# Adjacency blocks of a graph network: one-hots of one chunk between additions, weightings of four chunks, addresses read by threes

## The reference

```python
deg = jnp.maximum(segment_sum(ones, dst, 1250), 1.0)
x = x + L0(relu(layernorm(x)), src, dst, deg)               # mean over neighbours, two linear maps
x = x + L1(relu(layernorm(x)), edge_weight)                 # two graph convolutions
x = x + L2(relu(layernorm(x)), edge_attr_128)               # a message for each edge, summed, then a GRU
x = x + L3(relu(layernorm(x)), edge_weight1)                # weighted sum over neighbours, a linear map
```

## Time and profile before

| | |
|---|---|
| median of 3 runs | 1490.85 us (1489.72 to 1490.96) |
| profiled execution | 1488.92 us |
| its span in the profile | 1486.7 us |
| busy in the span | PE 88%, DVE 66%, POOL 48%, ACT 38% |
| mean granted clock of TensorE | 0.957 of full speed |
| first one-hot of the build to its last addition's start | 294.86 to 539.62 us |

### The profile page before, as it was taken

One profiled execution on the slowest core, in us unless ns is written; L12 is line 12 of the kernel. 1 busy time (PEld: TensorE's weight loads), 2 busy tenths in 40 slices (PEclk: granted clock), 3 DMA queues, 4 the chain that ended last, 5 costly groups with the idle time before them and its releaser, 6 DMA issues.

```text
span 1486.7 us, 19898 instructions
## 1 busy us (share of the span) xinstructions
PE 1309.6 (88%) x4184; PEld 685.9 (46%) x4184; DVE 988.1 (66%) x1719; ACT 565.0 (38%) x1438; POOL 719.2 (48%) x873
## 2 busy tenths in 40 slices
PE   5859898098888888959998899999998999997998
PEld 2534443043333333438874444444454444443775
DVE  8798253078888889841286388888896576667432
ACT  0211311066666620121011388888886221222210
POOL 0677777677777725766771266676663000000000
PEclk9989999599999999979999999999999999998999
DMA  8832522110000044443223577777775000000220
GB/s 337 322 118 65 191 66 79 46 57 18 19 21 16 9 181 156 121 154 96 89 81 127 161 224 215 228 227 225 227 221 184 20 1 0 1 0 18 71 89 34
DMA packets 87236, 167.86 MB, mean 113 GB/s; under 512 B 16108, under 2 KB 44654, under 8 KB 84628
## 3 DMA queue, kind: packets, MB, share of 16 engines
q1 hardware_dynamic: 59044, 102.19, 20.4%
q0 software_dynamic: 25472, 59.97, 13.2%
q10 hardware_dynamic: 2672, 5.11, 1.1%
HBM read 115.97 MB, written 51.25 MB: 112 GB/s over the span
## 4 chain that ended last, share of the span: by engine, by line
PE 45%; issue 17%; POOL 14%; DMA 13%; DVE 9%; POOLq 1%; ACT 1%; DVEq 1%; ACTq 0%
PE pb L1060 21%; DMA arena<-p_rows,gidx 11%; POOL cell_rows L671 8%; PE pb L1142 6%; PE pb L1168 6%; PE pb L1328 5%; PE pb L1176 2%; POOL tiles L725 2%; PE pb L1046 1%; POOL arena L725 1%; PE pb L1083 1%; PE pb L1258 1%; DMA cell_rows<-tiles,gidx 1%; DVE arena L1560 1%; POOL arena L784 1%
## 5 line engine op out<-in xcount | busy, mean ns | idle before, releaser
L784 POOL DMA_INDIRECT arena<-p_rows,gidx x184 | 191.5, 1041 | 67.3 <-issue 58.4
L717 POOL DMA_INDIRECT dst_rows<-ering,gidx x168 | 172.2, 1025 | 100.0 <-issue 71.4
L671 POOL DMA_INDIRECT cell_rows<-tiles,gidx x168 | 168.8, 1004 | 68.0 <-issue 39.7
L1258 PE MATMUL pb<-arena 128*128 128x512 f32 x368 | 191.6, 604 | 5.6 <-ACT arena L944 5.6
L1576 DVE TENSOR_TENSOR arena<-pb,arena 128x384 f32 x272 | 150.0, 552 | 45.8 <-PE pb L1142 24.4
L1060 PE MATMUL pb<-ws,tiles 128*128 128x512 f32 (+1 forms) x360 | 146.3, 554 | 12.0 <-ACT tiles L806 12.0
L1684 DVE TENSOR_TENSOR arena<-pb,arena 128x512 f32<-128x512 f32 x184 | 124.4, 686 | 41.6 <-DMA arena<-p_rows,gidx 39.5
L1142 PE MATMUL pb<-arena 128*128 128x384 f32 x272 | 107.5, 520 | 47.9 <-POOL arena L725 46.1
L847 ACT ACTIVATE arena<-iota,free 128x128 f32<-128x128 f32 x272 | 94.3, 393 | 123.4 <-PE pb L1142 82.4
L1142 PE MATMUL pb<-tiles,arena 128*128 128x384 f32 x272 | 106.2, 514 | 22.8 <-POOL tiles L725 21.0
L1060 PE MATMUL pb<-arena,tiles 128*128 128x512 f32 x240 | 103.9, 593 | 0.0
(11 more groups left out here) (258 smaller groups left out, 2129.8 us busy)
## 6 DMA issues: line engine op xcount, KB each, us to landing
dst_rows<-arena SPq DMA_DIRECT2D x6, 2046.0 KB, 17.5
ering<-in_edge_attr_dram SPq DMA_DIRECT2D x41, 256.0 KB, 3.0
arena<-adj SPq DMA_DIRECT2D x10, 640.0 KB, 3.8
arena<-dst_rows SPq DMA_DIRECT2D x24, 264.0 KB
arena<-wt_gru SPq DMA_DIRECT2D x48, 128.0 KB
ws<-dst_rows SPq DMA_DIRECT2D x22, 264.0 KB, 2.9
arena<-in_x_dram SPq DMA_DIRECT2D x18, 256.0 KB, 8.7
arena<-in_L_gnn_W_hh_dram SPq DMA_DIRECT2D x3, 1024.0 KB
```

Of the source, the lines that this page charges most:

```text
L671: nc.gpsimd.indirect_dma_start(cell_rows[:, :], bass.IndirectOffsetOnAxis(gidx[:, SPAN * a + k:SPAN * a + k + 1], 0), cring[:, a, k], None ...
L717: nc.gpsimd.indirect_dma_start(dst_rows[:, :], bass.IndirectOffsetOnAxis(gidx[:, k:k + 1], 0), ering[:, k, :], None).then_inc(e_scattered[ ...
L784: nc.gpsimd.indirect_dma_start(rows[:, k, :], None, p_rows[:, :], bass.IndirectOffsetOnAxis(gidx[:, k:k + 1], 0)).then_inc(g_landed[k], 16)
L1258: nc.tensor.matmul(e_bank(k)[:], erowT[:, k % 4], w1e_sb, start=True, stop=True).then_inc(edge_mm, 1)
```

## The change

One-hots are made one chunk at a time, eight ahead, one after each addition, and compared with a copy of the row 1 to 128 in PSUM bank 4 (`counting`), which nothing else uses during the build. DVE's loop runs over 16 chunks. Its addresses are read one at the start and then five times three, each behind an addition. POOL weights four chunks (`HALF`) in one instruction of 128 x 1024, and PE waits for it once in four chunks. A column is scattered after every second turn instead of in each; `EARLY` is 2, so 16 columns are scattered in the build and 152 behind it.

```diff
-EARLY = CELL_CHUNKS // TURN // COL
+HALF = TURN // 2
+EARLY = CELL_CHUNKS // TURN // (2 * COL)
...
             def weights_turn(i, with_column=None):
-                for q in range(TURN // 2):
-                    pool.wait_ge(dst_hot, TURN // 2 * i + q + 1)
+                for q in range(2):
+                    pool.wait_ge(dst_hot, TURN * i + HALF * (q + 1))
                     passed()
-                    hot = ohd(2 * q, 2)
...
+                    hot = ohd(HALF * q, HALF)
...
-                    if q == 1 and with_column is not None:
-                        scatter_column(with_column)
+                if with_column is not None:
+                    scatter_column(with_column)
...
-                    weights_turn(COL * i + k, k)
+                    weights_turn(2 * COL * i + 2 * k, k)
+                    weights_turn(2 * COL * i + 2 * k + 1)
...
                         if k % 2 == 0:
                             pe.wait_ge(src_hot, TURN // 2 * i + k // 2 + 1)
-                            pe.wait_ge(weighted, TURN // 2 * i + k // 2 + 1)
+                        if k % HALF == 0:
+                            pe.wait_ge(weighted, 2 * i + k // HALF + 1)
...
-            def hots(i, q):
-
-                at_least(dve, block_done, TURN * i + 2 * q - 6)
-                vtt(ohd(2 * q, 2)[:, :, 0], iota1[:].unsqueeze(1).to_broadcast([P, 2, P]),
-                    cellm[:, bass.ds(TURN * i + 2 * q, 2), 1:2].to_broadcast([P, 2, P]), ALU.is_equal).then_inc(dst_hot, 1)
+            def hot(i, k):
+
+                vtt(ohd(k % TURN, 1)[:, :, 0], counting.unsqueeze(1),
+                    cellm[:, bass.ds(2 * TURN * i + k, 1), 1:2].to_broadcast([P, 1, P]), ALU.is_equal).then_inc(dst_hot, 1)
...
             def turn(i, last):
-                at = table_values(cell_at[0:1, bass.ds(TURN * i, TURN)], (CELLS - 1) * P)
...
+                at = list(table_values(cell_at[0:1, bass.ds(2 * TURN * i, 1)], (CELLS - 1) * P))
+                for k in range(2 * TURN):
+                    add_block(i, k, at[k])
+                    if k % 3 == 0 and len(at) < 2 * TURN:
+                        at += table_values(cell_at[0:1, bass.ds(2 * TURN * i + k + 1, 3)], (CELLS - 1) * P)
+                    if not last or k < TURN:
+                        hot(i, k + TURN)
+
+            counting = pb[4][:, 0:P]
+            link(nc.vector.tensor_copy(counting, iota1[:]))
```

More of the change, by code:

```diff
@@ L720, in weights_turn @@
             def weights_turn(i, with_column=None):
-                for q in range(TURN // 2):
-                    pool.wait_ge(dst_hot, TURN // 2 * i + q + 1)
+                for q in range(2):
+                    pool.wait_ge(dst_hot, TURN * i + HALF * (q + 1))
                     passed()
-                    hot = ohd(2 * q, 2)
-                    nc.gpsimd.tensor_tensor(hot[:, :, 1:3], hot[:, :, 0:1].to_broadcast([P, 2, 2, P]),
-                                            cellm[:, bass.ds(TURN * i + 2 * q, 2), 2:4].unsqueeze(3).to_broadcast([P, 2, 2, P]),
+                    hot = ohd(HALF * q, HALF)
+                    nc.gpsimd.tensor_tensor(hot[:, :, 1:3], hot[:, :, 0:1].to_broadcast([P, HALF, 2, P]),
+                                            cellm[:, bass.ds(TURN * i + HALF * q, HALF), 2:4].unsqueeze(3).to_broadcast([P, HALF, 2, P]),
                                             ALU.mult).then_inc(weighted, 1)
-                    if q == 1 and with_column is not None:
-                        scatter_column(with_column)
+                if with_column is not None:
+                    scatter_column(with_column)
             def weights_and_edges(i):
@@ L742, in _ @@
                 weights_and_edges(i)
-            for i in range(COL * EARLY, CELL_CHUNKS // TURN):
+            for i in range(2 * COL * EARLY, CELL_CHUNKS // TURN):
                 weights_turn(i)
@@ L1570, in add_block @@
             def add_block(i, k, at):
-                n = TURN * i + k
+                n = 2 * TURN * i + k
                 dve.wait_ge(block_done, n + 1)
@@ L1578, in turn @@
             def turn(i, last):
-                at = table_values(cell_at[0:1, bass.ds(TURN * i, TURN)], (CELLS - 1) * P)
[L1580 to L1584, removed]
+                at = list(table_values(cell_at[0:1, bass.ds(2 * TURN * i, 1)], (CELLS - 1) * P))
[7 more added lines that the diff above has]
+            link(nc.vector.tensor_copy(counting, iota1[:]))
             dve.wait_ge(cells_loaded, 16)
             dve.wait_ge(wt_stored[0], 32)
-            turns = CELL_CHUNKS // TURN
-            for q in range(3):
-                hots(0, q)
+            turns = CELL_CHUNKS // (2 * TURN)
+            for k in range(TURN):
+                hot(0, k)
             turn(0, False)
```

## The result

| | before | changed |
|---|---|---|
| median (range), us | 1490.41 (1489.72 to 1490.96) | 1510.24 (1507.93 to 1511.71) |
| profiled execution, us | 1488.92 | 1510.29 |
| its span, us | 1486.7 | 1508.6 |
| first addition, us | 298.95 | 299.65 |
| last addition, us | 539.62 | 558.92 |

The ratio of the times is 1.0132 (95% interval 1.0114 to 1.0149): **slower**, by 19.8 us, where 7 us of gain were forecast. The last addition stands 19.3 us later, so nearly all of the loss arises in the build. Here are DVE's three kinds of work in the build by line, in the changed kernel (ns min/median/max, first and last start), with POOL's weighting behind them. They answer to the earlier trace rows.

What follows compares the result with a forecast made beforehand. DVE's row of additions was taken to set the build's pace; 298.95 + 1.0 + 229.2 + 3.4 put the last addition at 532.6 instead of 539.62, 7.0 us earlier, so 1484.0 us, range 1472 to 1493.

Steps and rivals of the forecast that it cites:

- Addresses by threes: DVE's address reads in the build: a read of three words was to take 0.39 us, bounds 0.30 and 0.60.
- An interval with a read: Between DVE additions with a three-word read and a one-hot between them: forecast 0.94 us, five a round.
- plain intervals: Between DVE additions with only a one-hot between them: forecast 0.75 us, ten a round.
- The chain's extra waits: Build, chain through one-hot, POOL's weighting and PE, 4.13 us: forecast to add 0.2 us a round, 3.4 in all.
- a read has a floor: Rival, DVE's address reads: three words cost 0.60 us like eight, 14.5 us added, time 1498.5; chance 0.10.
- One-hots of one chunk: DVE in the build: 272 one-hots instead of 136, 0.29 us each, wholly within time that was waited.
- The 1510 us: Time by the skill's instruction-cost table if none of the one-hots' 26 us more of DVE were covered.
- The row in PSUM: DVE's one-hots in the build: a PSUM source frees them from POOL, so 0.2 to 0.4 us lost a turn goes.
- the rival in which it does not: Rival: PSUM source does not free one-hots from POOL; up to 1 us each, some 60 us, 1545; chance 0.04.
- Weighting by fours: POOL in the build: one weighting of 1024 columns was to take 2.06 us, with next to no fixed part.
- The first rival: DVE's reads short or hidden: 1474, or near 1469 if the 4.13 us chain sets a round of 12.7; chance 0.12.
- The late columns: Sixteen columns moved behind the build: forecast to cost nothing, 7 us to spare; rival that they surface, 1484 to 1492, chance 0.04.

## Why the prediction was wrong

**The step that failed** is the price in "Addresses by threes": "by a line between them three take 0.39", with bounds of 0.30 and 0.60 from the reads of one and of eight words. Three words measured 0.745, above the upper bound. The line assumed that a read costs more with each word, from one to eight, at one rate. The runs show 0.22 for each further word wherever a read takes no whole group of four, and 0.04 for all three further words where it does. Eight words at 0.60 were cheap for their number, which fits two whole groups. Two points of the earlier trace rows could not show this, and the upper end was no bound: a read of fewer words can cost more than one of eight, which the forecast took as excluded without a reason in the rows.

Most of the working around this price held. An interval with a read was to be 0.12 + read + 0.17 + 0.26; with 0.745 that is 1.30, and the first one measured 1.30, the later ones 1.22 and 1.23. The second is longer, 1.40, for a longer read (below). Five such intervals take 6.37 us instead of 4.70, in 17 rounds 28.4 us. The rest of a round moved little: ten plain intervals sum to 7.57 instead of 7.50 (17 x 0.07 = 1.2 more), and its start takes 1.26 instead of 1.36 (1.7 less). That start is the read and 0.94 more in every kernel with single one-hots, from 1.25 with a read of 0.31 to 1.54 with one of 0.60; the forecast had 1.06 more. Rounds in which single intervals are longer than these medians add 2.0: together 17 x (15.32 - 13.56) = 29.9. The chain's extra waits of 3.4 us vanished, as longer intervals cover them, and the first addition came 0.7 instead of 1.0 later. 532.6 + 29.9 - 3.4 - 0.3 = 558.8; measured, 558.92.

A smaller slip made the forecast's gain look larger. It set rounds of plain intervals against the whole old build as measured. By the same plain intervals the old build takes 34 x 7.05 - 1.18 = 238.5 us and not 240.7. So 2.2 of the 7.0 us of gain came from longer turns that the forecast counted on the old side only; the new side turned out to have 2.0 us of them too.

**The rival "a read has a floor"** had the side and the place: six reads in DVE's row instead of two, decisive from 0.51 us a read. Its price of 0.60, and so its 1498.5, was too low, and its mechanism was not the right one: one word takes 0.30 in all these runs. What costs is the count and place of the words. With 0.745 in place of 0.60 its own formula, 85 x 0.355 - 3.4 = 26.8 us more, gives 1510.8, beside the 1510.24 measured; that it comes so close is in part luck, since the small terms that it leaves out nearly cancel.

The Trainium skill (page DMA: Bandwidth & Descriptors, section on latency) gives a floor of about 600 ns for a tensor_load. These runs contradict it as a floor: one word takes 0.30 us, four whole ones 0.34. Nor is it a typical price: reads reach 0.97 us.

**One-hots of one chunk**: 0.282 us measured, 0.29 said; their cost is covered, as said. DVE's busy time does grow: 136 one-hots of two chunks from PSUM take 56.3 us, 272 of one chunk 76.5. But the interval with a single one-hot is 0.76, where the pair of intervals with one double one-hot had 0.75 and 0.81. The rule of the Trainium skill that was weighed against this part (page VectorE: DVE Perf Modes, section on the TRN2 errata) makes instructions of 128 columns dear, 0.26 us by its table, close to the 0.28 measured. The 1510 us that the prediction worked out for it, with nothing covered, is the time measured only by chance: the same one-hots stand in the kernel with reads of eight, which takes 1474.56.

**The row in PSUM** freed the one-hots from POOL, as said; the rival in which it does not would have cost about 60 us, and the run with the row in SBUF shows 72.2.

**Weighting by fours** takes 1.90 instead of 2.06 us: by 2 x 1.04 - 1.90 about 0.18 of an instruction is fixed (an estimate), so "next to no fixed part" was off by that. The 3.4 us that the chain through POOL was to add can't be seen in the changed kernel, where the longer intervals cover them; with cheap reads, weighting by fours and by pairs end within 0.6 us of each other. The first rival, a round of 12.7 set by that chain alone, was reached by no run: the shortest is 13.20.

**The late columns** stayed hidden, but the margin of 7 us was taken on one path only. Timelines of POOL and SP in the changed kernel, against the earlier trace rows, with SP's stores of `p_rows` in the kernel before as the last line:

```profile
827.00 0.96 POOL L718 DMA_INDIRECT dst_rows<-ering,gidx  x1 [0.30 <-issue]
827.95 4.39 POOL L762 MEMSET arena<- 128x5120 f32 x1
...
817.88 0.32 SPq L522 DMA_DIRECT2D ering<-in_edge_attr_dram  x1
818.36 0.37 SPq L555 DMA_DIRECT2D arena<-in_L_gnn_b_dram  x1
...
826.63 14.66 SPq L587 DMA_DIRECT2D p_rows<-tiles  x5
841.76 0.94 SPq L576 DMA_DIRECT2D arena<-dst_rows  x2
```

```profile
804.88 13.32 SPq L586 DMA_DIRECT2D p_rows<-tiles  x5
```

The clear follows the last column at once: it had 20 us of idle time before. It ends at 832.34, before SP's row loads at 841.76, as forecast. What the forecast left out is SP's own order of work. SP issues the last loads of edge rows (to 817.88) before some loads of vectors and then the stores of `p_rows`, which so begin 21.8 later, 2.4 more than the build's end. SP's row loads stand 23.1 later, 3.8 more. The last of these stores and the messages nevertheless start 19.3 and 19.4 later, the same as the build: the delay was made up before them.

**Behind the messages** another 2.6 us are lost. The last addition into the sums is 19.3 later, DVE's first instruction of the GRU 21.9, the end 21.8. These are the stretches of the changed kernel, columns as in the earlier trace rows:

```profile
1155.00:1160.00 5.00, 5.00 (x17) 2.59 (x16) 3.85 (x7) 4.40 (x13) 2.71 (x3) 1.00 0.84 155
1160.00:1165.00 5.00, 2.37 (x7) 0.90 (x6) 4.68 (x9) 3.16 (x8) 0.00 (x0) 0.91 0.32 68
1165.00:1170.00 5.00, 4.06 (x11) 2.33 (x11) 2.02 (x4) 0.94 (x2) 0.00 (x0) 0.50 0.14 15
1170.00:1175.00 5.00, 5.00 (x16) 3.33 (x15) 4.90 (x4) 3.32 (x5) 0.00 (x0) 0.57 0.64 250
1175.00:1180.00 5.00, 5.00 (x13) 2.17 (x12) 0.03 (x1) 0.00 (x0) 0.00 (x0) 1.00 0.00 0
```

PE is busy for 2.37 of 5 us while the last edges are summed, then the granted clock falls to 0.50, the lower level of 1.2 GHz, for about 10 us in all (an estimate from the shares in these rows: 0.9 + 5.0 + 4.3). In the kernel before PE was busy for 2.90 of 5 us at the same passage (1145 to 1150 there), and the clock stayed at 1.00 (it had fallen to 0.53 earlier, from 1130 to 1135):

```profile
1145.00:1150.00 5.00, 2.90 (x13) 1.61 (x14) 3.36 (x6) 1.49 (x4) 0.00 (x0) 1.00 0.00 0
```

The change doesn't touch that stage and PE's work there is the same. It is one profiled execution of each, so it is observed and not tested. From the last addition of the build to the end the thirteen profiled executions of this case take 944.0 to 951.1 us, 947.1 before and 949.6 here, so 2.6 us lie within what that stretch varies by.

## What to carry to other kernels

A line through two measured sizes does not bound what lies between them: through one and eight words it said 0.39 for three, and the chip took 0.745. Read register tables in whole groups of four words from a place divisible by four, and if a count must change, measure that very read before a loop is built around it. When several parts come together, look for the one that carries the gain: here a single source moved to PSUM gives 12.4 of the 16.1 us that the whole change has to give, by the last additions of the profiled executions.

## What was not expected of the hardware

- A read of the address table into registers takes 0.30 us for one word, 0.52 for two, 0.745 for three and 0.96 for four words from an uneven place; four words from a place divisible by four take 0.34 and eight 0.60.
- A read can take longer a little behind a scatter. In the changed kernel's chain of waits and POOL's timeline, the second read of this round starts 0.17 us after the scatter ends:

```profile
375.91 0.75 DVEq L1567
...
378.72 0.87 DVEq L1567
```

```profile
377.54 1.01 POOL L718 DMA_INDIRECT dst_rows<-ering,gidx  x1 [0.15 <-issue]
```

  In the 14 rounds where a read starts within 0.3 us of a scatter's end it takes 0.78 to 0.89 us, and no other read of three takes over 0.77. With pairs and even fours a read that starts 0.45 to 0.5 us behind a scatter takes 0.36 to 0.41 instead of 0.34, and with pairs and reads of eight one that starts 0.13 to 0.15 behind takes 0.74 to 0.76 instead of 0.60. But reads that start only 0.06 behind one take their usual 0.60 in that kernel, and in the kernel before with reads of three those 0.03 to 0.07 behind take 0.75 to 0.78, against 0.75 to 0.89 some 0.3 behind. So it is no matter of being the first read after a scatter. It explains the interval of 1.40 among those of 1.22 to 1.30. Scatter and long read coincide; that the one causes the other was not tried.
- The first read of a kernel's build is longer by about 0.25 us: 0.609 for an even four, 0.555 for one word, 0.86 for eight.
- With both sources in SBUF, one-hots of 0.28 us that meet POOL's weighting last until 0.15 us behind its end, up to 1.99 us (all 66 that take over 0.4). With one source in PSUM they don't.
